# Attention's branch: two units in front of it, the heads' transposes inside it

## The reference

```python
latent_kv = (k + v) @ W_down_kv
k_rec, v_rec = latent_kv @ W_up_k, latent_kv @ W_up_v
scores = clip(einsum('bhqd,bhkd->bhqk', qh, kh) * scale)      # 16 heads of width 8
scores = clip(scores * exp(-0.0001 * abs(i - j)))             # decay over distance
out = einsum('bhqk,bhkd->bhqd', softmax(scores), vh)
return heads_side_by_side(out) @ Wo
```

## Time and profile before

| | |
|---|---|
| median of 3 runs | 796.51 us |
| the profiled execution, its own time | 798.54 us |
| its span, first to last instruction | 796.7 us |
| TensorE busy, share of span | 684.6 us, 86% |
| ScalarE busy | 557.8 us, 70% |
| VectorE busy | 482.7 us, 61% |
| GpSimd busy | 271.0 us, 34% |
| mean granted TensorE clock | 0.93 |

### The profile page before, as it was taken

How to read it: one execution, slowest core, us unless ns; L and a number is a source line. 1 busy time by engine, 2 the same in 40 slices (tenths; PEclk the granted TensorE clock), 3 DMA queues, 4 the chain that set the end, 5 groups by cost and what they waited for, 6 DMA issues and landing times.

```text
span 796.7 us, 11232 instructions
## 1 busy us (share of the span) xinstructions
PE 684.6 (86%) x3617; PEld 403.3 (51%) x3617; DVE 482.7 (61%) x1259; ACT 557.8 (70%) x789; POOL 271.0 (34%) x298
## 2 busy tenths in 40 slices
PE   2789788888888899999686669999999999999587
PEld 2566566666566667777464542332333223332465
DVE  4789878879778888888676532334422222222474
ACT  4557574666767575655444649999999999999143
POOL 3286456766656565555511600112000000000110
PEclk9999999999989999999858759999999999999757
DMA  9002232222223233333100398000199000000001
GB/s 263 5 1 69 82 95 89 92 87 86 85 79 95 80 102 112 111 116 119 53 1 0 70 194 160 2 1 1 24 185 197 20 1 1 1 1 1 2 1 53
DMA packets 31342, 54.53 MB, mean 68 GB/s; under 512 B 4624, under 2 KB 13280, under 8 KB 29776
## 3 DMA queue, kind: packets, MB, share of 16 engines
q1 hardware_dynamic: 30128, 53.38, 25.6%
q0 software_dynamic: 224, 0.34, 0.2%
q10 hardware_dynamic: 928, 0.06, 0.1%
HBM read 35.71 MB, written 1.28 MB: 46 GB/s over the span
## 4 chain that ended last, share of the span: by engine, by line
PE 34%; ACT 31%; issue 14%; DVE 13%; POOL 8%; ACTq 0%; DVEq 0%; POOLq 0%
ACT raw_w L830 26%; PE bank L1403 7%; PE bank L1404 6%; PE bank L1405 6%; POOL act_parts L570 4%; PE bank L1528 2%; PE bank L1525 2%; PE bank L1526 2%; PE bank L1443 2%; DVE act L1082 2%; POOL rstd L517 1%; DVE bank L1071 1%; PE bank L1700 1%; DVE up L1060 1%; ACT xt L659 1%
## 5 line engine op out<-in xcount | busy, mean ns | idle before, releaser
L830 ACT ACTIVATE raw_w<-bank,minus_c 128x1024 f32<-128x1024 f32 x256 | 259.6, 1164 | 5.6 <-DVE bank L1272 3.5
L570 POOL TENSOR_TENSOR act_parts<-act,act_parts 128x512 fp32r<-128x512 f32 x128 | 167.5, 1310 | 121.0 <-ACT act_parts L731 100.2
L1272 DVE TENSOR_TENSOR bank<-bank,fix 128x256 f32<-128x256 f32 x128 | 55.3, 433 | 181.4 <-PE bank L1684 181.4
L717 ACT ACTIVATE bank<-bank,b_gate 128x512 f32<-128x512 f32 x112 | 74.2, 662 | 112.7 <-PE bank L1405 62.2
L1403 PE MATMUL bank<-xn_parts,w_hi 128*128 128x512 f32 x256 | 109.3, 427 | 20.1 <-ACT bank L717 10.2
L1060 DVE TENSOR_SCALAR up<-bank,b_up 128x512 f32<-128x512 f32 x128 | 95.5, 746 | 36.7 <-PE bank L1405 33.0
L1405 PE MATMUL bank<-xn_parts,w_hi 128*128 128x512 f32 x256 | 102.2, 399 | 0.0
L1404 PE MATMUL bank<-xn_parts,w_lo 128*128 128x512 f32 x256 | 102.0, 399 | 0.0
L514 POOL TENSOR_SCALAR var_eps<-mean_var 128x4 f32<-128x4 f32 x28 | 7.2, 257 | 239.5 <-DVE mean_var L928 238.2
L1082 DVE SCALAR_TENSOR_TENSOR act<-up,bank 128x512 f32<-128x512 f32 x128 | 86.6, 677 | 0.0
L731 ACT ACTIVATE act_parts<-act 128x512 fp32r<-128x512 f32 x128 | 79.8, 623 | 4.2 <-DVE act L1082 4.2
(11 more groups left out here) (205 smaller groups left out, 1069.2 us busy)
## 6 DMA issues: line engine op xcount, KB each, us to landing
grow<-scores SPq DMA_DIRECT2D x68, 256.0 KB, 3.1
early<-scores SPq DMA_DIRECT2D x44, 256.0 KB, 3.2
raw_w<-in_gate_up SPq DMA_DIRECT2D x4, 512.0 KB, 9.0
w_lo<-gelu_parts SPq DMA_DIRECT2D x8, 256.0 KB, 5.3
w_lo<-act_parts SPq DMA_DIRECT2D x8, 256.0 KB, 5.4
w_hi<-gelu_parts SPq DMA_DIRECT2D x6, 256.0 KB, 4.5
w_hi<-act_parts SPq DMA_DIRECT2D x6, 256.0 KB, 5.5
x_tok<-in_x SPq DMA_DIRECT2D x4, 256.0 KB, 3.9
```

The source lines that it names most:

```text
L570: pool.tensor_tensor(act_lo[:, j % NACT, :], act[:, j % NACT, :], act_hi[:, j % NACT, :].bitcast(F32), ALU.subtract).then_inc(s["lo_ready" ...
L717: eng.activation(out, bank[:, G, :], ACT.Gelu_apprx_sigmoid, bias=b_gate[:, e:e + 1]).then_inc(s["glu_ready"], 1)
L830: eng.activation(probs[:, u % NP, :], pair, ACT.Exp, bias=minus_c[:, b:b + 1])\
```

## The change

`EARLY_UNITS = 2`: TensorE makes the scores of units 0 and 1 behind the transposes of the bound and ahead of the spreading of it, after waits for all copied values and all maxima. VectorE makes their two corrections behind the flag, ahead of its own read and branch. ScalarE reads the flag and branches first, and copies minus_c inside either branch; TensorE waits for minus_c inside too.

The heads' transposes, high parts and low parts are moved into the branches. In the fast one TensorE transposes chunk c once the normalizations that fill it are counted (`heads_whole(c)`: 7, 8, 15, 16 of 16), chunks 0 to 2 ahead of the last turn and chunk 3 behind the last normalization, into banks 2 to 5. VectorE makes low part 0 ahead of the last normalization and 1 to 3 behind it. The output products stay behind the branch and go to banks 0, 1, 6, 7; the additions follow without low parts between. The general branch gets the memset, the transposes and both parts at its end.

The core of the diff (`scores` leaves `attn_fast` with its text unchanged and is shown once):

```diff
 def heads_bank(c):
-    return c
+    return 2 + c
 def out_bank(c):
-    return 4 + c
+    return (0, 1, 6, 7)[c]
 BOUND = K_BANK[1]
...
     return 2 * (CH // 128) * (u // (2 * KB)) + 2 * (kb % (CH // 128)) + hp + 1
+EARLY_UNITS = 2
+def heads_whole(c):
+    return QC * G4 * (c // QC) + QC * (G4 - 1) + c % QC + 1
 SLOTS = 4
...
                .then_inc(s["exped"], 1)
+    def take_bound():
+        eng.wait_ge(s["neg_ready"], 1)
+        eng.activation(minus_c[:], bank[:, BOUND, 0:NB], ACT.Copy).then_inc(s["minus_c_ready"], 1)
+        eng.wait_ge(s["minus_c_ready"], 1)
     def attn_heads(b):
...
     def attention():
         attn_rest()
-        eng.wait_ge(s["neg_ready"], 1)
-        eng.activation(minus_c[:], bank[:, BOUND, 0:NB], ACT.Copy).then_inc(s["minus_c_ready"], 1)
-        eng.wait_ge(s["minus_c_ready"], 1)
         eng.wait_ge(s["flag_ready"], 1)
...
         with eng.If(fast):
+            take_bound()
             attn_fast()
+            for b in range(NB):
+                attn_heads(b)
         with eng.Else():
+            take_bound()
             eng.dma_start(gen_decays, io["decay"]).then_inc(s["gen_table"], 16)
             for b in range(NB):
                 attn_general(b)
-        for b in range(NB):
-            attn_heads(b)
+            for b in range(NB):
+                attn_heads(b)
     def attn_general(b):
...
         maxima(3)
+    def head_lo(c):
+        eng.wait_ge(s["ao_hi_ready"], c + 1)
+        eng.tensor_tensor(xn_lo[:, chunk(c)], bank[:, heads_bank(c), :], xn_hi[:, chunk(c)].bitcast(F32),
+                          ALU.subtract).then_inc(s["ao_lo_ready"], 1)
     def late_decay(i):
...
         eng.wait_ge(s["flag_ready"], 1)
+    def fix_scores(u):
+        g, qc, kb, hp = unit(u)
+        i = kb % (CH // 128)
+        turned = fix[:, None, :].to_broadcast([128, 2, 128])
+        pair = bank[:, 2 * (u % 3):2 * (u % 3) + 2, 128 * i:128 * (i + 1)]
+        eng.wait_ge(s["scored"], u + 1)
+        eng.tensor_tensor(pair, pair, turned, ALU.mult).then_inc(s["fixed"], 1)
     def attn_fast():
...
         for u in range(NB * UNITS):
             g, qc, kb, hp = unit(u)
-            if kb // (CH // 128) == qc:
-                i = kb % (CH // 128)
-                turned = fix[:, None, :].to_broadcast([128, 2, 128])
-                pair = bank[:, 2 * (u % 3):2 * (u % 3) + 2, 128 * i:128 * (i + 1)]
-                eng.wait_ge(s["scored"], u + 1)
-                eng.tensor_tensor(pair, pair, turned, ALU.mult)\
-                    .then_inc(s["fixed"], 1)
+            if u >= EARLY_UNITS and kb // (CH // 128) == qc:
+                fix_scores(u)
             if 0 < u <= UNITS and u % (UNITS // G4) == 0:
...
         take_out(NB * G4 * QC - 1)
+        head_lo(0)
         normalize(NB * G4 * QC - 1)
+        for c in range(1, NC):
+            head_lo(c)
     def attn_general(b):
...
                 eng.memset(spare1[:], 0.0).then_inc(s["group_done"], 1)
-    def attn_heads(b):
-        for c in range(QC * b, QC * (b + 1)):
-            eng.wait_ge(s["ao_hi_ready"], c + 1)
-            eng.tensor_tensor(xn_lo[:, chunk(c)], bank[:, heads_bank(c), :], xn_hi[:, chunk(c)].bitcast(F32),
-                              ALU.subtract).then_inc(s["ao_lo_ready"], 1)
     def attn_out(b):
...
         attn_bound()
+        for u in range(EARLY_UNITS):
+            fix_scores(u)
         fast = eng.value_load(small_scores[0:1, 0:1], min_val=0, max_val=1)
...
             attn_general(1)
-        eng.memset(tops[:, 0, 0:1], 0.0).then_inc(s["ao_ready"], 1)
+            eng.memset(tops[:, 0, 0:1], 0.0).then_inc(s["ao_ready"], 1)
+            for c in range(NC):
+                head_lo(c)
         for b in range(NB):
-            attn_heads(b)
             attn_out(b)
...
           .then_inc(s["neg_ready"], 1)
-        pe.wait_ge(s["v_copied"], NC)
-        pe.wait_ge(s["minus_c_ready"], 1)
+    def scores(u):
+        g, qc, kb, hp = unit(u)
+        b = u // UNITS
+        if u % (UNITS // G4) == 0:
+            pe.wait_ge(s[f"stack{g}_loaded"], stacks_in(g, b))
+        before = min(max(128 * kb - CH * qc, 0), CH)
+        if u >= 3:
+            pe.wait_ge(s["exped"], u - 2)
+        for side, first, end in ((1, 0, before), (0, before, CH)):
+            for a in range(2):
+                if first < end:
+                    j = 2 * hp + a
+                    rows = slice(32 * j, 32 * (j + 1))
+                    last = pe.matmul(bank[:, 2 * (u % 3) + a, first:end],
+                                     k_stack[g][rows, side, 128 * kb:128 * (kb + 1)],
+                                     q_stack[g][rows, side, CH * qc + first:CH * qc + end],
+                                     start=True, stop=True, tile_position=(32 * j, 0))
+        last.then_inc(s["scored"], 1)
+    def head_in(c):
+        for t in range(TPC):
+            last = pe.transpose(bank[:, heads_bank(c), 128 * t:128 * (t + 1)], x_tok[:, TPC * c + t, :],
+                                ident[:])
+        last.then_inc(s["ao_t_ready"], 1)
     def attn_fast():
...
         def weigh(t):
...
         for t in range(steps + 2):
-            if t < steps:
+            if EARLY_UNITS // 2 <= t < steps:
                 scores(2 * t)
...
                 weigh(t - 2)
-            if t < steps:
+            if EARLY_UNITS // 2 <= t < steps:
                 scores(2 * t + 1)
...
                 turn(t // KB - 1)
+        pe.wait_ge(s["exped"], NB * UNITS - 1)
+        for c in range(NC - 1):
+            pe.wait_ge(s["normed"], heads_whole(c))
+            head_in(c)
         turn(NB * G4 * QC - 1)
+        pe.wait_ge(s["normed"], heads_whole(NC - 1))
+        head_in(NC - 1)
     def attn_general(b):
...
                 last.then_inc(s["gen_pv"], 1)
-    def attn_heads(b):
-        pe.wait_ge(s["ao_ready"], 1)
-        for c in range(QC * b, QC * (b + 1)):
-            for t in range(TPC):
-                last = pe.transpose(bank[:, heads_bank(c), 128 * t:128 * (t + 1)], x_tok[:, TPC * c + t, :],
-                                    ident[:])
-            last.then_inc(s["ao_t_ready"], 1)
     def attn_out(b):
...
         attn_bound()
+        pe.wait_ge(s["v_copied"], NC)
+        pe.wait_ge(s["maxes_ready"], NC)
+        for u in range(EARLY_UNITS):
+            scores(u)
         attn_spread()
...
         with pe.If(fast):
+            pe.wait_ge(s["minus_c_ready"], 1)
             attn_fast()
         with pe.Else():
+            pe.wait_ge(s["minus_c_ready"], 1)
+            pe.wait_ge(s["fixed"], EARLY_UNITS)
             for b in range(NB):
                 attn_general(b)
-        for b in range(NB):
-            attn_heads(b)
+            pe.wait_ge(s["ao_ready"], 1)
+            for c in range(NC):
+                head_in(c)
         for b in range(NB):
...
```

More of the change, by code:

```diff
@@ L1666, in attn_spread @@
                   .then_inc(s["neg_ready"], 1)
-                pe.wait_ge(s["v_copied"], NC)
-                pe.wait_ge(s["minus_c_ready"], 1)
-            def attn_fast():
[L1671 to L1682, removed]
-                                rows = slice(32 * j, 32 * (j + 1))
-                                last = pe.matmul(bank[:, 2 * (u % 3) + a, first:end],
-                                                 k_stack[g][rows, side, 128 * kb:128 * (kb + 1)],
-                                                 q_stack[g][rows, side, CH * qc + first:CH * qc + end],
-                                                 start=True, stop=True, tile_position=(32 * j, 0))
-                    last.then_inc(s["scored"], 1)
```

## The result

The changed kernel takes 790.5 us, median of 20 runs (787.1 to 800.08), against 796.23 us for the kernel before in 20 runs beside it. The ratio is 0.9931, 95% interval 0.9911 to 0.9950: 5.5 us less by the ratio and 5.7 by the medians, where 5.9 were forecast. The profiled execution took 787.95 us with a span of 786.1, the kernel before 798.54 and 796.7.

A forecast was written before the change was run, and what follows sets the result against it. ScalarE's exponentials bound attention's inside, so only the time before the first and after the last could move. Front 2.1 plus tail 3.8 made 5.9 us, from the median 796.51 to 790.6 us; forecast 789.3 to 792.0, range 788.3 to 793.3.

The forecast's parts named there:

- The front: From the flag to the first exponential: early scores and the copy inside bring it to 471.4, gain 2.1 us.
- I take 2.2, the only one measured: ScalarE's entry, reading the flag and branching, taken as TensorE's 2.2 us; bounded above by 3.50 us.
- wait for the power: Before attention: scores of units 0 and 1 take 0.8 us, done by 468.8, before GpSimd's power at 469.17.
- The tail: From the last exponential to the last addition, which ends at 747.3 against 751.11: gain 3.8 us.
- TensorE's exit: Leaving the branch before the output products: taken as VectorE's 2.84 us, at most 3.6, from the last transposes' issue.
- sign of being wrong: In the tail: wrong if TensorE's first product is over 3.2 us behind its last transposes.
- The products: Twelve matmuls of the four output products run unbroken, two thirds at half clock: 4.5 us.
- The normalization's delay: In the tail: transposes and low part 0 ahead of the last normalization make it end 0.7 us later.
- start of the exponentials: First exponentials, TensorE at half clock: left unchanged, with a possible loss of 0.5 us or return of up to 1.1.
- last stage: Unedited stage after attention: clock may rise up to 3 us earlier or later; taken as 0, within 1.4 us.
- The slow rivals: Slow entry: ScalarE needs 3.50 us, 791.9 us, 8 in 100; slow exit: TensorE's is 3.6, 792.1 us, 9 in 100.
- slower: Behind attention TensorE never regains full clock, doubling 10.0 us of work: 800.6 us, 3 in 100.

The follow-up runs named there:

- read-only kernel: Full change with the fast path alone, no branch or general path; each of three engines still reads the flag but does not use it: 784.84 us, ratio 0.9892.
- fill: Change with last stage inside both branches plus 37 extra matmuls computing nothing: 784.84 us; a lighter one with 33 and three early units: 787.12 us.
- tail-only kernel: Kernel before with only the tail part: heads' transposes and low parts inside the branch, front as before; 794.09 us, ratio 0.9979.
- stage inside: Full change with the output products, additions and whole last stage also inside both branches: 787.33 us, ratio 0.9909.
- without a branch: Full change with the fast path alone: no read of the flag, no branch, general path left out; 782.83 us, ratio 0.9834.
- front only: Kernel before with only the front part: early units 0 and 1, minus_c copied inside; heads, low parts and additions behind the branch; 792.55 us, ratio 0.9961.
- order only: Kernel before with one edit: VectorE makes all four low parts ahead of all four additions, everything behind the branch; 793.68 us, ratio 0.9984.

## Why the prediction was right

**The whole.** 790.6 forecast, 790.5 measured; the ratio's interval, applied to 796.5, is 789.4 to 792.5. Both parts gained, by the steps that the prediction names. That the sum fits to 0.1 us is luck: by the means over the profiles the front gave 1.0 us more than forecast and the tail 1.2 less.

**The front** was 2.1 us and measured 3.2 (2.4 to 3.6 over the profiles). The step that was off is "I take 2.2, the only one measured" for ScalarE's entry: from the flag to the copy it was 1.20 us in the changed kernel and 1.25 to 2.00 in the seven others that copy inside. I had called a shorter entry possible and left it out of the bounds, though nothing excluded it. The prediction priced read and branch together; that the read is nearly all of it only the read-only kernel shows. The claim that scores of two units fit into the wait for the power holds: 464.41 + 0.50 against a product at 465.78.

**The tail** was 3.8 us and measured 3.1 between the two profiles, 1.9 to 3.3 over all. The step that was off is TensorE's exit, taken as VectorE's 2.84 from the issue of the last transposes: from their first row (731.83) to the first product it is 3.85, and 3.64 to 3.70 in the two other profiles of this tail. From their end it is 3.19, just within the 3.2 that I had named as a sign of being wrong. VectorE's exit was not the longer one, since its first addition waited for the first product. The products took 4.6 us from the first one's start, where 4.5 were forecast with two thirds at half clock; eight of twelve were. The normalization's delay was taken a little too large: from VectorE's copy (729.31) to the normalization's end (731.78) it is 2.47 us, against 2.02 in the earlier trace rows, so 0.45 instead of 0.7. About half of the gain is the order on VectorE, which the prediction named only in its reading of the earlier trace rows (the additions ahead of low parts 2 and 3) and did not price apart.

**The clock.** No change was taken for the start of the exponentials (261.33 for 261.65, right) and for the last stage (45.09 for 45.59, within the 1.4). No row had stood behind the 3 us by which the rise in the last stage could move; over all profiles without a fill the time at half there went from 17 to 30.5 us. Outside the account fell also the unedited stretch ahead of attention, 3.4 us between two profiles. The slow rivals, and "slower", did not occur; the clock came back in every profile.

**What the copy inside is worth** was not split in the prediction; alone it is 0.3 to 0.7 us.

## What to carry to other kernels

An engine's read of a flag into a register has no row of its own, but it takes time. Here ScalarE's copy came 1.2 to 2.0 us behind the flag and TensorE's scores 1.2 to 2.5 us behind its small product, against 0.8 and 0.7 without a read. It belongs ahead of, or beside, the chain that the flag comes from. The branch behind it added nothing visible on the way in and 2.6 to 3.2 us on the way out, so short dependent work behind a branch is better put inside it: that took 4.7 us out of this tail, of which about 1 us came back at the end. Look at the order of short instructions on an engine that serves two loops before moving anything: eight of them reordered gave 1.6 of the tail's 3.1 us. Where single executions differ by more than the effect, cut both profiles at the same events and compare stretches, with the granted clock beside each.

## What the runs showed that I had not expected

The spread of single runs goes with the clock's. Over the 163 runs of all kernels that the ratios keep, a common line for the device time, with an offset for each kernel, falls by 4.2 us for each 0.01 of mean granted clock and leaves 1.1 us. (Far off it stood one run of the tail-only kernel, 847.96 us at a mean clock of 0.745; its like was not seen again.) At a mean clock of 0.938 it gives 794.9 for the kernel before, 792.8 and 792.6 for front and tail alone, 790.7 and 790.9 for the full change, 787.7 with the stage inside and 785.2 without a branch. For the two fills it gives 791.0: their times rest on a higher clock. It is a way to compare, not a cause: an edit can move the clock too.

The exit of a branch costs twice, by its wait and by the clock that falls in it: 4.7 us in the tail, of which TensorE's idle time is 3.2. Beside it stand fetches in the instruction queues of the changed kernel, from 732 to 736 us:

```profile
q14 instruction: 2, 0.02, 1.7%
q8 instruction: 1, 0.02, 1.6%
```

The kernel before has three such packets as well, from 737 to 742 us; the earlier trace rows shows one of them, since its window is shorter. From 726 to 742 us front only, tail only and order only have five, and the two kernels without a branch have two, with no wait beside them. So some three packets go with the exits. How much of the wait is the fetch was not taken apart.

The best version that keeps both paths is the change with the last stage inside the branches: 787.1 to 787.3 us, ratio 0.9898 to 0.9909, with intervals that overlap that of the change. The one with 37 idle matmuls has a lower median, 784.84, with an interval that overlaps both.
